# Scaling and summing the messages of a graph layer: one-hots built three units ahead, the first message group of each unit scaled by GpSimd instead of by VectorE

## The reference

```python
alpha = jax.nn.softmax(a, axis=0)                 # over all edges, 8 heads
alpha_mean = alpha.mean(axis=1, keepdims=True)    # one weight per edge
agg = segment_sum(msg * alpha_mean, dst, num_segments=6250)
out = node_features + agg @ W_out                 # then a layer norm
```

## Time and profile before

| | |
|---|---|
| median of 3 runs | 3296.63 us |
| the profiled execution's own time | 3297.24 us |
| its span, first to last instruction | 3295.4 us |
| busy in the span: PE, DVE, ACT, POOL | 84%, 72%, 53%, 55% |
| mean granted clock of TensorE, of full speed | 0.959 |
| `layer1_aggregate`, first scaling to last add | 2854.3 to 3231.6 us of the span |

### The profile page before, as it was taken

How to read it: one execution, slowest core, us unless ns; L and a number is a source line. 1 busy time by engine, 2 the same in 40 slices (tenths; PEclk the granted TensorE clock), 3 DMA queues, 4 the chain that set the end, 5 groups by cost and what they waited for, 6 DMA issues and landing times. The chain is left out here.

```text
span 3295.4 us, 84558 instructions
## 1 busy us (share of the span) xinstructions
PE 2777.1 (84%) x20718; PEld 2224.7 (68%) x20718; DVE 2381.8 (72%) x5243; ACT 1741.5 (53%) x3923; POOL 1827.3 (55%) x1957
## 2 busy tenths in 40 slices
PE   0769888988888898844999999999999999567764
PEld 0368888888888888822666766667666667455554
DVE  5589999999999999984455555555555555688786
ACT  6334444444444444443555555555555555566664
POOL 0077777777777777503777777777777776000001
PEclk9879999999999999966999999999999999799997
DMA  2588877888887888514787888888888887355552
GB/s 71 136 223 224 220 214 210 220 217 219 216 218 215 217 219 217 150 54 126 235 239 237 235 239 238 238 238 237 237 236 239 237 237 225 99 161 161 162 160 59
DMA packets 598133, 653.61 MB, mean 198 GB/s; under 512 B 90491, under 2 KB 477175, under 8 KB 598072
## 3 DMA queue, kind: packets, MB, share of 16 engines
q1 hardware_dynamic: 438854, 302.67, 33.8%
q0 software_dynamic: 89088, 243.39, 27.1%
q10 hardware_dynamic: 70130, 106.88, 9.7%
HBM read 565.19 MB, written 121.55 MB: 208 GB/s over the span
## 5 line engine op out<-in xcount | busy, mean ns | idle before, releaser
L1279 POOL DMA_INDIRECT l_G<-rows_d,l_sidx x928 | 878.3, 946 | 361.0 <-issue 263.2
L870 POOL DMA_INDIRECT l_G<-rows_d,l_sidx x928 | 902.9, 973 | 299.7 <-issue 272.4
L1409 ACT ACTIVATE l_h<-l_H,l_cols 128x512 f32<-128x512 f32 x464 | 317.6, 685 | 508.5 <-PE l_H L1316 492.8
L966 ACT ACTIVATE l_e<-l_A 128x512 f32<-128x512 f32 x232 | 138.5, 597 | 614.2 <-PE l_A L900 609.7
L946 PE MATMUL l_accp<-l_ohe,H 128*128 128x128 f32 x3712 | 453.1, 275 | 0.0
L946 PEld LDWEIGHTS l_accp<-l_ohe,H 128*128 128x128 f32 x3712 | 434.0, 192 | 0.0
L1473 DVE TENSOR_TENSOR l_SC<-l_SC,l_b 128x512 f32<-128x512 f32 x232 | 162.2, 699 | 356.0 <-PE l_SC L1345 356.0
L1636 PE MATMUL ag_accp<-ag_msg,ag_pick 128*128 128x128 f32 x1856 | 266.5, 289 | 140.4 <-DVE ag_pick L1678 130.5
L1636 PEld LDWEIGHTS ag_accp<-ag_msg,ag_pick 128*128 128x128 f32 x1856 | 227.0, 193 | 179.9 <-DVE big L1708 114.2
L1345 PEld LDWEIGHTS l_SC<-big,l_h 128*128 128x128 f32 x1856 | 238.9, 191 | 132.9 <-issue 132.9
L1619 ACT ACTIVATE ag_msg<-ag_msg,ag_alpha 128x128 f32<-128x128 f32 x812 | 261.1, 390 | 118.1 <-DMA ag_msg<-msg_d 107.8
(11 more groups left out here) (189 smaller groups left out, 5793.3 us busy)
## 6 DMA issues: line engine op xcount, KB each, us to landing
msg_d<-l_msg ACTq DMA_DIRECT2D x232, 256.0 KB
ag_msg<-msg_d SPq DMA_DIRECT2D x232, 256.0 KB, 2.7
l_fd<-dst_d SPq DMA_DIRECT2D x464, 96.0 KB
l_pd<-dst_d SPq DMA_DIRECT2D x464, 96.0 KB
l_in<-ea_d SPq DMA_DIRECT2D x464, 80.0 KB
l_lo<-mark_d SPq DMA_DIRECT2D x464, 64.0 KB
l_G<-rows_d,l_sidx POOLq DMA_INDIRECT x1856
l_code<-code_d SPq DMA_DIRECT2D x464, 64.0 KB
```

The lines of the kernel that those rows point to most:

```text
L870: nc.gpsimd.indirect_dma_start(out=G[:, s, j, :], out_offset=None, in_=rows_d[0][:, :], in_offset=bass.IndirectOffsetOnAxis(ap=sidx[:, hal ...
L1279: nc.gpsimd.indirect_dma_start(out=G[:, s, j, :], out_offset=None, in_=rows_d[1][:, :], in_offset=bass.IndirectOffsetOnAxis(ap=sidx[:, hal ...
L1409: nc.scalar.activation(out_t[:, s % 2, :], in_p[:, :], ACT.Silu, bias=cols[:, col:col + 1]).then_inc(ready, 1)
```

## The change

The group that VectorE scaled in even units goes to GpSimd, which now scales group 0 of every unit, with a `tensor_tensor` product against `alpha` broadcast along the row. ScalarE scales groups 1 to 3 of every unit, VectorE none. The one-hots are built three units ahead. TensorE waits for one semaphore more, `beside`, which GpSimd raises.

```diff
-            OWN = [TJ - 1 + s % 2 for s in range(U)]
-            SHARED = [sum(OWN[0:s + 1]) for s in range(U)]
-            PICKED = [sum(2 + TJ - n for n in OWN[0:s + 1]) for s in range(U)]
...
+                beside = sem("ag_beside", st)
...
+                        pool.wait_ge(s_alpha, 1)
+                        al = alpha[:, (HEADS - 1) % 2, :]
+
+                        def step(lap, u):
+
+                            i, s, lp = item(lap, u)
+                            if not exists(i, NI):
+                                return
+                            pool.wait_ge(ld[s], 16 * (lp + 1))
+                            mine = msg_t[:, s, 0, :]
+                            nc.gpsimd.tensor_tensor(mine, mine, al[:, bass.ds(i * TJ, 1)].to_broadcast([P, C]),
+                                                    ALU.mult).then_inc(beside, 1)
+                        run_items(pool, step)
...
-                            for j in range(TJ - OWN[s], TJ):
+                            for j in range(1, TJ):
...
-                            pe.wait_ge(shared, lp * SHARED[-1] + SHARED[s])
-                            pe.wait_ge(pick_ready, lp * PICKED[-1] + PICKED[s])
+                            pe.wait_ge(shared, (TJ - 1) * (i + 1))
+                            pe.wait_ge(beside, i + 1)
+                            pe.wait_ge(pick_ready, 2 * (i + 1))
...
-                        dve.wait_ge(s_alpha, 1)
-                        al = alpha[:, (HEADS - 1) % 2, :]
...
-                        def weigh(lap, u, d):
-
-                            i, s, lp = item(lap, u, d)
-                            if not exists(i, NI) or OWN[s] == TJ:
-                                return
-                            dve.wait_ge(ld[s], 16 * (lp + 1))
-                            mine = msg_t[:, s, 0, :]
-                            nc.vector.tensor_scalar(mine, mine, al[:, bass.ds(i * TJ, 1)], None,
-                                                    ALU.mult).then_inc(pick_ready, 1)
...
                             add(lap, u, 0, 0, at[0])
-                            picks(lap, u, 2, 0)
-                            weigh(lap, u, 2)
+                            picks(lap, u, 3, 0)
                             follows = where_to(lap, u + 1) if u + 1 < U else None
                             add(lap, u, 0, 1, at[0])
                             at[0] = follows
-                            picks(lap, u, 2, 1)
+                            picks(lap, u, 3, 1)
```

## The result

The changed kernel takes 3236.81 us (median of 4 runs, 3236.39 to 3238.58), beside 3294.82 us for the kernel before in the same comparison. The ratio is 0.9826, interval 0.9809 to 0.9843: 58 us faster. The forecast was 3246.5 us, 50 us faster.

What follows compares the result with a forecast made beforehand. The prediction took engines waiting for each other, through one-hots only two units ahead, as the bound. From 3297.24 us, 73.3 less and 23.2 for collisions gave 3247.1, and 0.6 less for the median 3246.5 us; range 3218 to 3290.

Steps and rivals of the forecast that it cites:

- The wait goes: VectorE's adds: with one-hots three units ahead, the 0.34 us wait for PE in every second unit ends.
- The scaling goes: VectorE, every second unit: the scaling taken off it saves 0.26 us.
- VectorE's own lap: VectorE becomes the next bound: 8 units take 10.37 us, 1.296 us a unit, 300.7 us for 232 units.
- The turn: VectorE's branch and register load at a lap's end: between 0 and 0.65 us, taken as 0.40.
- The collision: One-hots with two SBUF inputs stand still while GpSimd's product runs: 0.10 us a unit, 23.2 us, bounds 0 to 0.39.
- The phase: Loads land 0.34 us into a step, so GpSimd's product gets the wide 0.45 us gap between one-hots, at price 0.
- No collision: Rival: every product fits the wide gap between one-hots, at no price; 3223 us, chance 0.20.
- The path is taken: Slower rival: products delay each unit's first or second one-hot by the whole 0.39 us, 90.5 us; 3314 us, chance 0.12.
- A longer product: Rival: GpSimd's product takes 0.67 us, not 0.39, costing 0.28 us a unit, 65 us; 3288 us, chance 0.12.
- PE becomes the bound: Rival: PE's extra wait and register arithmetic make a unit 1.48 us; 3266 us, chance 0.07.
- GpSimd's start: The library switch before the first product, up to 6.9 us, costs nothing, with 2.9 us of cover.
- The one-hots' mean: Sign in the profile: 419 ns rises to about 469 as forecast, stays 419 without collision, 615 at full price.

Runs made afterwards that it cites:

- a_depth3: The kernel before with one-hots three units ahead, VectorE still scaling the first group of even units; 3253.11 us, ratio 0.9893.
- c_narrow: The changed kernel with GpSimd's product of a unit also waiting for the second one-hot of that unit; ratio 0.9833 to the kernel before.
- d_turn: The changed kernel with VectorE's loop alone passing over two laps of 8 units at a time; 3225.81 us, ratio 0.9794 to the kernel before.
- b_noprod: The changed kernel without GpSimd's products and TensorE's wait for them, each unit's first group left unscaled; ratio 0.9830 to the kernel before.
- h_two: The changed kernel with GpSimd scaling the first two groups of each unit, ScalarE the other two; ratio 0.9839 to the kernel before.

## Why the prediction was right

The time, the direction and the mechanism were right: depth ends the wait, VectorE becomes the bound, the stage was forecast at 327 us and is 321. But two terms of the sum were mis-sized, by +17 and -23 us, and they nearly cancelled: that the stage came out within 6 us is in part luck.

- **The wait goes.** Right. Of the 20.1 us that the profile still puts down to TensorE, 14.2 stand at the turns and 4.5 at the register load right behind (0.24 us at 3008.51), a gap of 0.66 us with and without products. There the load ran from 3007.93 to 3008.27 and the add followed 0.24 us later, so it is no wait for sums either. The depth alone gives 1.25 us a lap, where 4 x 0.34 = 1.36 was the term.
- **The scaling goes**, 0.26 us each: too high. On top of the depth, the four scalings of a lap are worth 11.78 - 11.08 = 0.70 us, 0.18 each. The register load does not hide them: in a_depth3 the gap with a scaling and no load is 0.53 us where 0.34 is usual, 0.19 more, and the three with both are 0.24 longer on average. Of these 0.92 us a lap another gap and the turn, both shorter, take back 0.20. The 0.26 was read at one place.
- **VectorE's own lap**, 10.37 us: too low, measured 11.06. The turn lay at its upper bound (0.66, taken 0.40), and the load's gap was read at one favourable place (0.53, mean 0.594). The stage without collisions was forecast at 304 us and is 321: 17 us.
- **The collision**, 0.10 us a unit, 23.2 us: too high. The stretching exists, 7 us, and the trace shows its two handovers, but it costs nothing here. Four steps failed. The product needs the path for 0.26 us, not 0.39. The product is the one that waits twice as often (118 times, one-hots 58): its mean is 484 ns against a least of 394. The phase was not one: behind the first add of a step the products start at 0.12 to 0.74 us (medians by the unit of a lap), where I had 0.34 for all. And I let each stretched one-hot lengthen the lap, while the gaps with a register load took most of it back.
- **The rivals.** No collision, at 0.20, is what came to pass in the time it costs; its 3223 us were missed by the size of VectorE's lap. "The path is taken" has nothing left for it: when forced (c_narrow), the product waited. "A longer product": its floor, 394 ns, is the 0.39 us from the two rows, with the broadcast operand and the register's address. Two rows always lie on a line, so that was no evidence before the run. "PE becomes the bound": d_turn runs at 10.79 us a lap, below the changed kernel's.
- **GpSimd's start.** Right: the switch was issued at 2840.0, and the first product started at 2849.84, as soon as the weights were there.
- **Signs in the profile.** The one-hots' mean was to be 469 ns and is 434; I had named 419 with a long stage as the sign that turns or loads are it, and b_noprod shows just that. The releaser ahead of the adds, which I wanted to ask then, names the wrong engine. I had also written that the prediction fails if a product takes over 0.6 us; 40 of the 232 did, up to 0.70, all of them by waiting for a one-hot. The sign was meant for the product's own length and did not set the wait apart.

The Trainium skill, "SBUF — State Buffer", "Who interferes with whom", says that the order of issue decides who blocks. The traces agree in both directions: one-hots stretched to 0.51 us, products to 0.64. In 113 of the change's 118 waiting products the one-hot had been issued first; in the other five the product came second though its record starts 1 to 26 ns ahead. The prediction said that no row showed a product held by a one-hot: these do. For the time of this kernel it did not matter who waited.

## What to carry to other kernels

When a producer runs only one consumer's length ahead, deepen the ring first: that was 36 of the 56 us of the stage, and without it the scalings taken off VectorE gave only 12. Before pricing work that is moved to an idle engine, ask whether the bounding engine is bound by its instructions or by what stands between them: here VectorE was idle 46 of the 321 us (321.30 - 275.16), at register loads and turns, so that ScalarE, GpSimd and even leaving the work out gave the same time. Average a gap over a whole lap before it goes into a sum of 232 of them.

## What the runs showed that was not expected

- The turn of this 8-unit loop on VectorE, with a register load in it, stands 0.66 us above a usual gap with and without GpSimd's products, and the profile names TensorE as its releaser. In a doubled pass 0.47 us of it go; the pass of 16 units saved 9.2 us over 14 turns, and is the fastest of these kernels (0.9794).
- A register load on VectorE takes 344 ns for four values in a row, 598 for eight, 512 for two with a step. The step costs more than the two values left out save.
- GpSimd's product and VectorE's one-hot need their common path for only the last 0.26 and 0.28 us of 0.39 and 0.41, so a product can pass in a gap shorter than itself: in h_two one issued at 3158.82 took 0.40 us between one-hots issued at 3158.52 and 3159.08, and both kept their 0.41 to 0.42.
